# Expert stages: rows reach the experts' slots by 0/1 matmuls on TensorE, not by scatter and load; chunks of whole batches

## What is computed

```python
logits = einsum('btc,ce->bte', x, router_w) + router_b          # 8 experts
cap = int(LOAD_FACTOR * K * Tt // E)                            # 76 slots a batch and expert
top_k_logits, expert_indices = top_k(logits, K)                 # K = 2, of one batch
expert_probs = softmax(top_k_logits)
pos = cumsum(one_hot, axis=0) * one_hot - 1                     # all first choices, then all second
expert_inputs = buf.at[ei.ravel(), pos.ravel()].add(repeat(x, K))  # (8, 76, 128); over cap: dropped
h = einsum('eti,eih->eth', einp2, w_c_fc) + b_c_fc              # 128 -> 512
g = einsum('eti,eih->eth', einp2, w_gate) + b_gate
o = einsum('eth,eho->eto', silu(h * g), w_c_proj) + b_c_proj    # 512 -> 128
return sum(expert_probs[..., None] * o[i, p])                   # the two rows of a token
# x = x + 0.5 * that, on the layer-normed x
```

## Time and profile before

| | us |
|---|---|
| median of three runs (lowest, highest) | 2738.7 (2730.96, 2742.22) |
| the profiled execution, its own time | 2738.68 |
| its span, first to last instruction | 2736.9 |
| expert stage one, in that span | 514.9 to 1224.5 |
| expert stage two | 2037.8 to 2736.9 |

### The profile page before, as it was taken

The page is one execution under the profiler, slowest core; times in us unless marked ns, Lnnn a source line. Parts: engine busy times, 40 slices in busy tenths (PEclk is TensorE's granted clock), DMA queues, the critical chain, the costliest instruction groups (busy, mean ns, idle before and its releaser), DMA issues.

```text
span 2736.9 us, 44615 instructions
## 1 busy us (share of the span) xinstructions
PE 2259.9 (83%) x13878; PEld 1743.4 (64%) x13878; DVE 1361.3 (50%) x4152; ACT 1283.6 (47%) x2551; POOL 593.3 (22%) x687
## 2 busy tenths in 40 slices
PE   4979989667597789739999999999976668679974
PEld 3979979566354456536777777777765545345654
DVE  5867767543242334435555655556553324243443
ACT  3755557533232344426666666666643324234432
POOL 2112210133523433240000000000003351542234
PEclk9999999778797899969999999999996889789987
DMA  6070000011111122110000000000001111212222
GB/s 222 0 265 27 0 0 0 8 39 44 49 51 51 55 60 61 51 37 1 0 0 0 0 0 0 0 0 0 0 2 30 41 53 46 68 51 68 72 55 73
DMA packets 123488, 108.01 MB, mean 39 GB/s; under 512 B 14524, under 2 KB 103092, under 8 KB 123008
## 3 DMA queue, kind: packets, MB, share of 16 engines
q1 hardware_dynamic: 105952, 77.05, 9.0%
q0 software_dynamic: 16384, 27.68, 4.0%
q10 hardware_dynamic: 1056, 2.10, 0.3%
HBM read 51.86 MB, written 60.82 MB: 41 GB/s over the span
## 4 chain that ended last, share of the span: by engine, by line
PE 42%; another core or an unknown queue 4%; issue 4%; DVE 2%; ACT 2%; POOL 0%; DMA 0%; ACTq 0%; POOLq 0%; DVEq 0%; SPq 0%
PE moe_bank L1517 5%; PE lin_bank L982 4%; PE moe_bank L1531 4%; PE moe_bank L1521 4%; PE lin_bank L902 4%; PE lin_bank L910 4%; PE lin_bank L929 4%; PE lin_bank L921 4%; PE lin_bank L958 3%; PE lin_bank L974 2%; PE lin_bank L945 1%; PE moe_bank L1507 1%; DVE moe_act L1683 0%; DVE all_x L1701 0%
## 5 line engine op out<-in xcount | busy, mean ns | idle before, releaser
L1587 ACT ACTIVATE moe_fc<-moe_bank,all_b_fc 128x512 f32<-128x512 f32 (+3 forms) x448 | 244.6, 549 | 679.8 <-PE moe_bank L1517 330.9
L1517 PE MATMUL moe_bank<-moe_rowsT,all_w_fc 128*128 128x512 f32 (+3 forms) x896 | 386.0, 515 | 152.4 <-ACT moe_fc L1587 73.7
L1683 DVE SCALAR_TENSOR_TENSOR moe_act<-moe_bank,all_b_moe_gate,moe_fc 128x512 f32<-128x512 f32 (+3 forms) x448 | 255.9, 577 | 430.3 <-PE moe_bank L1521 207.4
L1521 PE MATMUL moe_bank<-moe_rowsT,all_w_gate 128*128 128x512 f32 (+3 forms) x896 | 372.9, 500 | 24.1 <-issue 18.0
L1435 POOL DMA_INDIRECT rows_in<-moe_xn,moe_put_at x256 | 250.0, 977 | 580.6 <-DVE moe_put_at L1671 506.3
L1445 POOL DMA_INDIRECT moe_landed<-rows_out,moe_take_at x256 | 256.1, 1000 | 481.7 <-issue 269.1
L1517 PEld LDWEIGHTS moe_bank<-moe_rowsT,all_w_fc 128*128 128x128 f32 x896 | 165.4, 213 | 242.1 <-issue 101.2
L1531 PE MATMUL moe_bank<-all_w_proj,moe_act 128*128 128x128 f32 x2432 | 305.2, 282 | 16.9 <-issue 15.8
L1531 PEld LDWEIGHTS moe_bank<-all_w_proj,moe_act 128*128 128x128 f32 x2432 | 294.4, 199 | 17.0 <-issue 15.7
L1521 PEld LDWEIGHTS moe_bank<-moe_rowsT,all_w_gate 128*128 128x128 f32 x896 | 175.8, 212 | 164.2 <-issue 122.8
L1692 DVE TENSOR_TENSOR moe_expert_out<-moe_bank,all_b_proj 128x512 f32<-128x512 f32 (+3 forms) x112 | 58.1, 519 | 388.0 <-remote 230.9
(11 more groups left out here) (214 smaller groups left out, 3749.0 us busy)
## 6 DMA issues: line engine op xcount, KB each, us to landing
moe_rows<-rows_in SPq DMA_DIRECT2D x48, 256.0 KB
rows_out<-moe_expert_out SPq DMA_DIRECT2D x48, 256.0 KB
rows_in<-all_zeros SPq DMA_DIRECT2D x1, 9728.0 KB, 28.1
rows_out<-all_zeros SPq DMA_DIRECT2D x1, 9728.0 KB, 53.2
rows_in<-moe_xn,moe_put_at POOLq DMA_INDIRECT x256
moe_landed<-rows_out,moe_take_at POOLq DMA_INDIRECT x256
moe_rows<-rows_in SPq DMA_DIRECT2D x16, 192.0 KB
rows_out<-moe_expert_out SPq DMA_DIRECT2D x16, 192.0 KB
```

The lines of the kernel that those rows point to most:

```text
L1517: nc.tensor.matmul(bank[FC + j % 2][:, 0:c.width], k.w_fc[:, e, j * P:(j + 1) * P], rowsT[:, i % 2, 0:c.width], start=True, stop=True).the ...
L1521: nc.tensor.matmul(bank[GATE + j % 2][:, 0:c.width], k.w_gate[:, e, j * P:(j + 1) * P], rowsT[:, i % 2, 0:c.width], start=True, stop=True) ...
L1587: nc.scalar.activation(fc[:, j, 0:c.width], bank[FC + j % 2][:, 0:c.width], ACT.Identity, bias=k.b_fc[:, e * MC + j:e * MC + j + 1]).then_ ...
L1683: nc.vector.scalar_tensor_tensor(act_in[:, i % 2, j, 0:c.width], bank[GATE + j % 2][:, 0:c.width], k.b_moe_gate[:, e * MC + j:e * MC + j + ...
```

## The change

Chunks are now whole batches, (2, 3, 5, 5, 5, 5, 5, 2), that is 152, 228, 380 and 152 rows an expert; 64 units. A unit's last block may be short: `down` runs it at full width on cleared columns of `act_in`, and `keep` stores it by a second DMA.

`scatter`, `rows_in`, `load`, `transpose_rows` and `copy_rows` are gone. In their place, for each batch: GpSimd's `split` makes three bf16 parts of `xn`, whose sum is exactly `xn`; `assign` also makes `slot`, the number 1 to 608 of expert and position; GpSimd's `first_choice` compares `slot_ids` (1 to 608) with the first choice's slot of each token, and VectorE's `second_choice` adds the comparison with the second, which gives `hot`, a 0/1 matrix of 128 tokens by 608 slots for each tile. TensorE's `send` multiplies the parts by `hot`, half of the experts (304 columns) at a time, into one PSUM bank: the rows come out transposed, in their slots. ScalarE's `land` copies them to `rowsT`, which now holds all experts of two chunks.

Masks, counts and assignments are made batch by batch. Each chunk routes the batches of the next one, a batch every 5 slots (9 in chunks 0 and 6), its steps at the lags of `ROUTE_LAGS`. GpSimd's list now follows the slots too, with each gather 5 slots ahead of its combine. `slot_ids` is made in the setup stage; the GAU stage fills `rows_out` alone.

The diff, cut to its core:

```diff
-CHUNKS = (128, 256, 512, 512, 512, 384, 128)
-ROUTE_IN = {0: ((1, 0, 2), (2, 14, 2)), **{c: ((c + 2, 2, 3),) for c in range(1, len(CHUNKS) - 2)}}
-COMBINE_IN = {1: (29, 1), 2: (14, 2), 3: (12, 2), 4: (12, 2), 5: (7, 3), 6: (17, 8)}
+CHUNKS = (2, 3, 5, 5, 5, 5, 5, 2)
+ROUTE_STEP = (9, 5, 5, 5, 5, 5, 9)
+COMBINE_IN = {1: (14, 6), 2: (11, 6), 3: (11, 5), 4: (11, 5), 5: (11, 5), 6: (11, 5), 7: (12, 6)}
+ROUTE_LAGS = {"norm": 0, "transpose": 1, "router": 2, "mask": 3, "count": 4, "assign": 5, "hot0": 8, "hot1": 9,
+              "send0": 10, "send1": 11}
+GATHER_LEAD = 5
...
+            if c.n + 1 < len(plan):
+                for i, b in enumerate(plan[c.n + 1].batches):
+                    for what, lag in ROUTE_LAGS.items():
+                        work[i * ROUTE_STEP[c.n] + lag][what] = b
...
+                first, gap_of = COMBINE_IN[c.n]
+                for i, b in enumerate(plan[c.n - 1].batches):
+                    if first + i * gap_of < len(work):
+                        work[first + i * gap_of]["combine"] = b
+                        work[first + i * gap_of - GATHER_LEAD]["gather"] = b
...
+                    if c.whole:
+                        sp.dma_start(dst[e, c.first:c.first + c.whole * P, :].rearrange("(j p) d -> p j d", p=P),
+                                     expert_out[:, i % 2, 0:c.whole, :]).then_inc(kept[i % 2], 16)
+                    if c.left:
+                        sp.dma_start(dst[e, c.first + c.whole * P:c.first + c.width, :],
+                                     expert_out[0:c.left, i % 2, c.whole, :]).then_inc(kept[i % 2], 16)
...
+                def split(b):
+
+                    pool.wait_ge(xn_ready, b + 1)
+                    if b >= PARTS:
+                        pool.wait_ge(sent_ps, 2 * (b - PARTS) + 2)
+                    part = [parts[:, b % PARTS, q, :, :] for q in range(3)]
+                    x = xn[:, b % XN, :, :]
+                    link(nc.gpsimd.tensor_copy(part[0], x))
+                    link(nc.gpsimd.tensor_tensor(rest[:, :, :], x, part[0], ALU.subtract))
+                    link(nc.gpsimd.tensor_copy(part[1], rest[:, :, :]))
+                    nc.gpsimd.tensor_tensor(part[2], rest[:, :, :], part[1], ALU.subtract).then_inc(split_done, 1)
+                    pool.wait_ge(split_done, b + 1)
+
+                def first_choice(b):
+                    pool.wait_ge(routed, b + 1)
+                    if b >= 2:
+                        pool.wait_ge(sent_ps, 2 * (b - 2) + 2)
+                    for t in range(TILES):
+                        nc.gpsimd.tensor_scalar(hot[:, b % 2, t, :], k.slot_ids[:, :], slot[:, b % 2, t, 0:1], None,
+                                                ALU.is_equal).then_inc(hot_first, 1)
...
+                nc.gpsimd.memset(act_in[:, :, :, :], 0.0).then_inc(cleared, 1)
+                for b in plan[0].batches:
+                    split(b)
+                for b in plan[0].batches:
+                    first_choice(b)
+                for c, slots in order:
+                    for s, work in slots:
+                        if "norm" in work:
+                            split(work["norm"])
+                        if "assign" in work:
+                            first_choice(work["assign"])
+                        if "gather" in work:
+                            if work["gather"] == plan[c.n - 1].batches[0]:
+                                rows_kept(plan[c.n - 1])
+                            gather(work["gather"])
+                rows_kept(plan[-1])
+                for b in range(BATCHES):
+                    if b not in mixed:
...
+                def send(b, h):
+
+                    if h == 0:
+                        pe.wait_ge(split_done, b + 1)
+                        pe.wait_ge(hot_sb, TILES * (b + 1))
+                    if b or h:
+                        pe.wait_ge(sent_sb, 2 * b + h)
+                    for t in range(TILES):
+                        for q in range(3):
+                            last = nc.tensor.matmul(bank[SENT][:, 0:HALF], parts[:, b % PARTS, q, t, :],
+                                                    hot[:, b % 2, t, h * HALF:(h + 1) * HALF],
+                                                    start=(t == 0 and q == 0), stop=(t == TILES - 1 and q == 2))
+                    last.then_inc(sent_ps, 1)
...
+                    if j == 0 and e % 4 == 0:
+                        pe.wait_ge(sent_sb, 2 * c.batches[-1] + 1 + e // 4)
...
+                def land(b, h):
+                    c = chunk_of(b)
+                    j = b - c.batches[0]
+                    act.wait_ge(sent_ps, 2 * b + h + 1)
+                    if c.n >= 2:
+                        act.wait_ge(gate_ps, MC * EXPERTS * (c.n - 1))
+                    nc.scalar.copy(rowsT[:, c.n % 2, 4 * h:4 * h + 4, j * CAP:(j + 1) * CAP],
+                                   bank[SENT][:, 0:HALF].rearrange("p (e s) -> p e s", e=4)).then_inc(sent_sb, 1)
...
+                    link(nc.vector.scalar_tensor_tensor(o, top_atf[:, b % 2, :, :], float(CAP), o, ALU.mult, ALU.add))
+                    nc.vector.scalar_tensor_tensor(take_at[:, i:i + TILES, :], p, float(CAP), base[:, b % 2, :, :], ALU.min, ALU.add)
+                    nc.vector.scalar_tensor_tensor(s, p, float(CAP), o, ALU.min, ALU.add).then_inc(routed, 1)
...
+                def second_choice(b, t):
+                    dve.wait_ge(hot_first, TILES * b + t + 1)
+                    dve.wait_ge(routed, b + 1)
+                    nc.vector.scalar_tensor_tensor(hot[:, b % 2, t, :], k.slot_ids[:, :], slot[:, b % 2, t, 1:2], hot[:, b % 2, t, :],
+                                                   ALU.is_equal, ALU.add).then_inc(hot_sb, 1)
```

More of the change, by code:

```diff
@@ L1321, in moe_stage @@
         xn_ready = k.sem("xn_ready")
+        step = k.sem("split_step")
+        split_done = k.sem("parts_ready")
         xT_ps = k.sem("xT_in_psum")
@@ L1533, in down @@
                     last.then_inc(down_ps, 1)
-                for b in routing(0):
-                    transpose_x(b)
-                    if b:
-                        router(b - 1)
-                router(routing(0)[-1])
-                count(0)
-                transpose_rows(0)
+                for part in (transpose_x, router, count):
+                    for b in plan[0].batches:
+                        part(b)
+                for b in plan[0].batches:
+                    for h in range(2):
+                        send(b, h)
+                pe.wait_ge(cleared, 1)
                 for c, slots in order:
@@ L1551, in _ @@
                             count(work["count"])
-                        if s % MC == MC - 1:
-                            if i + 1 < UNITS:
-                                transpose_rows(i + 1)
-                            if i:
-                                down(i - 1)
+                        for h in range(2):
+                            if f"send{h}" in work:
+                                send(work[f"send{h}"], h)
+                        if s % MC == MC - 1 and i:
+                            down(i - 1)
                 down(UNITS - 1)
@@ L1594, in silu @@
                     nc.scalar.activation(a, a, ACT.Silu).then_inc(act_sb, 1)
-                for b in routing(0):
-                    copy_xT(b)
-                tanh(0)
-                copy_rows(0)
+                for part in (copy_xT, tanh):
+                    for b in plan[0].batches:
+                        part(b)
+                for b in plan[0].batches:
+                    for h in range(2):
+                        land(b, h)
                 for c, slots in order:
@@ L1607, in _ @@
                             tanh(work["count"])
[L1608 to L1613 removed]
+                        for h in range(2):
+                            if f"send{h}" in work:
+                                land(work[f"send{h}"], h)
+                        if s % MC >= 2:
+                            silu(i, s % MC - 2)
             @block.vector
@@ L1708, in combine @@
                         stats_of(k, b, t)
-                for b in routing(0):
-                    normalise(b)
-                    if b:
-                        choose(b - 1)
-                choose(routing(0)[-1])
-                choose_masks(0)
-                assign(0)
+                for part in (normalise, choose, choose_masks, assign):
+                    for b in plan[0].batches:
+                        part(b)
+                for b in plan[0].batches:
+                    for t in range(TILES):
+                        second_choice(b, t)
+                dve.wait_ge(cleared, 1)
                 for c, slots in order:
@@ L1728, in _ @@
                             assign(work["assign"])
+                        for t in range(TILES):
+                            if f"hot{t}" in work:
+                                second_choice(work[f"hot{t}"], t)
                         if "combine" in work:
```

286 lines of the change are left out of this document (112 added, 174 removed).

## The result

The changed kernel takes 2517.3 us, median of four runs, where the kernel before takes 2740.0 beside it: ratio 0.919, 95% interval 0.917 to 0.922. Forecast were 2520 us, range 2440 to 2690. The profiled execution has a span of 2512.8 us and took 2514.8.

The account below looks back on a forecast made before the run. Bound: TensorE standing in the expert stages' middles beside long runs of GpSimd's indirect DMAs. Startup, middle and tail, 23 + 546 + 25.5 and 23 + 546 + 26.5, save 219 us of 2736.9: forecast 2520 us, range 2440 to 2690.

Parts of the forecast that it names:

- `send` at 0.130 us: TensorE in the middle: each 304-column bf16 matmul takes 0.130 us, x 384 = 50 us more a stage.
- TensorE's sum of 487: Middle of an expert stage: 440 minus 17 for row transposes, plus 50 for `send` and 14 for `down`, in us.
- 32 for hand-offs: Middle: per-batch mask, count, assign, hot columns and sends cost 1.0 us a batch, 32 us; bounds 6 and 80.
- The residual stall: Gathers left in chunks 6 and 7: runs of 12 and 16 lose 9 and 13 us, 22 a stage; bounds 0 and 40.
- length less 8 us: Long runs of GpSimd's indirect DMAs cost about their length less 8 us; runs of four next to nothing.
- Startup: Expert stage before its first up matmul: 23 us, against 25.6 in the kernel before.
- the fourth rival: VectorE and GpSimd hold each other off: 12 us for every five batches, 77 a stage, 2674 us; chance 0.05.
- Tails: End of each expert stage: batches 29, 30 and 31 gathered after the last store, 5.2 us; tails 25.5 and 26.5.
- Late first choice: GpSimd's comparison takes 3.4 us, so the first choice comes late: 55 us a stage, 2630 us; chance 0.11.
- By the piece: Gathers cost 0.85 us a DMA whatever the run: 82 us a stage more, 2684 us; chance 0.10.
- GpSimd the bound: At 7.2 us a comparison GpSimd needs 22 us a batch: stage 752 us, whole 2834; chance 0.04.
- Runs not the cause: The 224 and 213 us stay and only added work counts, +47 - 3 + 5 a stage: 2837 us; chance 0.03.

Follow-up runs that it names:

- before_paced: The kernel before, all DMAs kept, from chunk 2's scatters each batch's four indirect DMAs wait for their own slot and combines move; 2472.5 us, ratio 0.894.
- send_one: The changed kernel with one bf16 part sent instead of three, the parts still made; 2470.5 us on a chip with the stall.
- both_on_vector: The changed kernel with both comparisons of a batch on VectorE, GpSimd left with splits and gathers; 2592.9 us on a chip with the stall.
- before_probe: The kernel before with added runs of 4, 8, 12 and 16 indirect DMAs in its second FFN stage; 2370.3 us on a chip without the stall.

## Why the prediction was right or wrong

**What bounded the kernel: right on the chip it was read from, and shown there.** Long runs of indirect DMAs on GpSimd stopped TensorE (busy for 2.94 of 10 us within one); breaking them in part (`before_paced`) brings back three quarters of the loss. That the forecast came true for the time is also luck of the place: the result was measured where the stall is, and the prediction had no term for a chip without it, where the same change takes 5.5% longer. **The size was too large.** The prediction took the bare sum of spacings, 440 us, for a middle without stalls, so 224 and 213 us for the stall. It is 192.6 and 183.0: the old middle without stalls is 471, 31 us over the sum, of which the prediction had seen rows (units of 12.2 us where the sum gives 12.0) only in the wide chunks. This doesn't enter the forecast, which builds the new middle up from its own terms.

**Terms of the new middle.** `send` at 0.130 us: six start at 853.16 in the changed kernel's second trace and the next `up` at 853.93, 0.128 each. `down` has its 2688 records. TensorE's sum of 487 plus 32 for hand-offs and 5 for the clock is 524; measured without stalls 530.6. Right to 7 us, though the first units don't run at the lower clock as before: from 540.5 to 550 it is granted at 0.50 in the kernel before and from 540.4 to 550 at 1.00 in the changed kernel; and `send_one` shows that three tenths of the send's price were hidden behind other waits, so that the send and the hand-offs aren't separate terms. **The residual stall: half.** 22 us predicted, 11.4 measured. The run of 12 in chunk 6, priced at 9, cost nothing (that chunk takes 69.36 us with the stall and 69.35 without); the 16 of chunk 7, priced at 13, cost 11.4. These windows of chunk 7 answer the windows of the earlier trace rows, first on the chip with the stall, then on one without:

```profile
1038.00:1048.00 10.00, 6.43 (x47) 5.75 (x45) 3.33 (x10) 3.09 (x8) 7.63 (x8) 0.97 0.24 59
1048.00:1058.00 10.00, 6.69 (x30) 5.61 (x28) 2.18 (x7) 1.58 (x4) 7.57 (x9) 0.67 0.20 49
```

```profile
1038.00:1048.00 10.00, 7.29 (x54) 6.79 (x54) 5.14 (x16) 4.62 (x12) 7.66 (x8) 0.96 0.25 62
1048.00:1058.00 10.00, 10.00 (x71) 9.65 (x70) 5.20 (x16) 4.49 (x13) 7.78 (x8) 0.87 0.27 68
```

So "length less 8 us" holds as a sum over many runs and not for each of them. Added over the runs of the middles as the traces have them, it gives 196 us for stage one of the kernel before (192.6 measured) and 47 and 42 for `before_paced` (523.1 and 526.5 less 471.1 and 469.6: 52.0 and 56.9 measured, 11 and 13 of them in the unpaced chunk 0); for the changed kernel 20.5 (11.4 measured). Taken singly, 12 in a row cost 0 in chunk 6, and 16 in a row 9 (FFN stage), 11 (chunk 7) and 11 to 13 (chunk 6 of `both_on_vector`). In the wide chunks of the changed kernel, with fours alone, nothing is lost: 77.3 us with the stall and without. What makes a run of 12 cost nothing there, no run here tells.

**Startup: wrong by 3 us.** 26.0 for 23. The largest term is one that the prediction put at nothing: "the clear of `act_in` lies under the norm". GpSimd's memset runs from 514.40 to 517.06, and VectorE's second operation of the norm, which took 0.20 us in the kernel before, ends with it and takes 2.34 (the two rows of the changed kernel, then the same operation before):

```profile
514.40 2.66 POOL L1465 MEMSET moe_act<- 128x3072 f32 x1 [123.77 <-POOLq L319]
514.77 2.34 DVE L234 TENSOR_SCALAR moe_mean<-moe_mean 128x74 f32<-128x74 f32 x1
```

```profile
515.22 0.20 DVE L232 TENSOR_SCALAR moe_mean<-moe_mean 128x74 f32<-128x74 f32 x1
```

The same happens in stage two (2.35 us). It makes 2.1 of the 3 us. The others are smaller: the first mask takes 0.67 us and not 0.19 beside GpSimd's subtraction; a comparison takes 1.79 us and not 1.55, twice ahead of the first `send`; and VectorE's second choice takes 1.29 to 1.35 us and not 0.85 as long as GpSimd compares beside it. First, second and fourth of its rows:

```profile
529.82 1.29 DVE L1705 SCALAR_TENSOR_TENSOR moe_hot<-all_slot_ids,moe_slot,moe_hot 128x608 bf16<-128x608 f32 x1
531.54 1.35 DVE L1705 SCALAR_TENSOR_TENSOR moe_hot<-all_slot_ids,moe_slot,moe_hot 128x608 bf16<-128x608 f32 x1 [0.43 <-POOL moe_hot L1447]
...
535.09 0.85 DVE L1705 SCALAR_TENSOR_TENSOR moe_hot<-all_slot_ids,moe_slot,moe_hot 128x608 bf16<-128x608 f32 x1 [0.43 <-POOL moe_hot L1447]
```

The last has no comparison beside it and takes 0.85. So the holding off of the fourth rival exists, to which the prediction gave a chance of 0.05, and it costs 2 to 3 us where VectorE's work is waited for, at the start. It doesn't have the price of 77 us a stage: the combine's mean goes from 406 to 350 ns when the comparisons leave GpSimd, 14 us over the whole kernel, on an engine with slack.

**Tails: wrong by 2 to 3 us.** Counted as in the earlier trace rows, to the next stage's first instruction or to the end of the span, they are 22.7 and 24.2 us instead of 25.5 and 26.5 (the windows above end at VectorE's last instruction, 0.6 and 2.3 us earlier). The four DMAs more came: VectorE's last instruction in stage one stands 22.1 us behind the last `down`, in the kernel before 16.2. But 4 us of the old 20.3 lay behind that instruction, and in the changed kernel 0.6 do. This isn't the stall: the kernel before has the same wait on a chip without it (first VectorE's first instruction behind stage one in the kernel before, then the list of waits of `before_probe`):

```profile
1224.87 0.77 DVE L1153 COPY lin_pick_last_row<-all_ident 128x128 f32<-128x128 f32 x1 [4.45 <-remote]
```

```profile
DVE lin_pick_last_row L1179 <- remote: 4.4, 1, 4.4
```

What ends that wait, and why the change shortens it, the traces don't show.

Together startup, middle and tail give 590.7 and 595.0 us where 594.5 and 595.5 were forecast. In stage one the errors are +3.0, -4.0 and -2.8, in stage two +3.7, -1.9 and -2.3: they partly cancel.

**Rivals.** Late first choice: VectorE waits for GpSimd's comparison 3.9 us in all; out. By the piece: out, `before_paced` has every piece and most of the time back. GpSimd the bound: busy 297 of 542 us. Runs not the cause: out on chips with the stall, and exactly what happens on the others. Its +49 us a stage (47 - 3 + 5) for work added has the sign of what they show, some 63 us a stage: half of 2492.8 - 2366.3. How a run of indirect DMAs holds TensorE up, the traces show only in part. In the kernel before TensorE starts the next unit's products right behind the `down` of the earlier trace rows, 12.7 us ahead of the `bias_out` that waits for it:

```profile
729.34 1.02 PE L1517 MATMUL moe_bank<-moe_rowsT,all_w_fc 128*128 128x512 f32 x2
```

That fits counts that arrive late and not operands that do. It isn't shown beyond that, as the profile models the ends of matmuls.

**What stays open.** Why two chips have the stall and two don't (the chip of the first result isn't known; its times are those of the former), and whether a chip keeps its condition: only one was met twice, without the stall both times. In the pages of runs with the stall the column from issue to landing is empty for the gathers; without it the row has it:

```profile
moe_landed<-rows_out,moe_take_at POOLq DMA_INDIRECT x256, 2.7
```

It is empty because many of the events that record DMA completions are missing in those traces: the changed kernel's has 5305 with the stall and 7881 without. Whether the missing records have to do with the cause or are one more effect, no run here tells. SP's 40 DMAs, issued in 19.2 us where GpSimd issues one every 1.3 us, cause no stall.

## What to carry to other kernels

If engines stand still with "remote" as the releaser while GpSimd issues indirect DMAs one after another, part them first: a wait for a slot count in front of every four gave 0.894 here, and a version of it cost nothing where there was no stall (0.996), while moving the scatter to TensorE gave 0.919 and cost 5.5% there. Before a redesign is built around a stall, measure the kernel on more than one chip. Work that seems too slow for its engine may be what parts a run of DMAs; ask what closes up when it is moved (chunk 6 took 82.2 us for 69.4 when the comparisons left GpSimd). And before work on an idle engine is put at nothing, ask what its neighbour does at that moment: a clear "under the norm" cost 2.1 us a stage.

## What the runs showed of the hardware that was not expected

- The same kernel takes 2361 to 2368 us on two chips and 2731 to 2771 in sessions on others, with undisturbed wide units of the changed kernel equal to within 0.05 us; the difference lies beside runs of indirect DMAs. Within a session the times of one kernel mostly repeat to 0.5%.
- On a chip with the stall TensorE's granted clock falls after it has stood, to 0.66 and 0.67 in the ten-microsecond windows above, a mix of stretches at 0.50 and at 1.00 (in the changed kernel TensorE is busy for 0.09 of the 2 us from 1044, and the clock is 0.50 from 1048 to 1054). Six products of `send` take 1.68 us at 533.04, in the startup, where the clock is 0.50, and 0.94 at 853.71, where it is 1.00; so what runs at 0.50 behind a stall should take longer too, which is an estimate from these two.
- A comparison of 608 f32 columns into bf16 takes 1.79 us at least on GpSimd (median 1.81) and 0.53 on VectorE (median).
- VectorE's operation on 4 columns (L1695 in the changed kernel) takes 0.16 us alone and 0.68 in nine of the ten cases where it starts at most 0.01 us behind the start of GpSimd's subtraction of 0.67; where it starts up to 0.03 us ahead of that, it keeps its 0.16 (median beside an indirect DMA 0.35). An operation on 74 columns takes 0.20 us alone and 2.34 where it starts 0.4 us behind a memset of 2.66.
